# Quaternion product in a fused fp32 transformer block: four last sums joined into two, and a new order of the steps

## What is computed

```python
x = L0_attn_x
xn = _layernorm(x)
x = x + _L0_attn_ref(xn, ...) + _L0_ffn_ref(xn, Wg, Wu, Wd)      # linear attention + FFN; 8 dense experts
xn = _layernorm(x)
x = x + _L1_attn_ref(xn, ...) + _L1_ffn_ref(xn, ...)             # 4 "quaternion" layers; top-2 of 8 experts
```

```python
qk = _hamilton(_to_quaternion(q), _to_quaternion(k))
qkv_p = _hamilton(qk, _to_quaternion(v))
# _hamilton(a, b), part by part:
a0*b0 - a1*b1 - a2*b2 - a3*b3
a0*b1 + a1*b0 + a2*b3 - a3*b2
a0*b2 - a1*b3 + a2*b0 + a3*b1
a0*b3 + a1*b2 - a2*b1 + a3*b0
```

## Time and profile before

| | |
|---|---|
| median of 3 runs | 1518.19 us (1517.88 to 1524.01) |
| the profiled execution | 1522.51 us |
| its span, first to last instruction | 1520.7 us |
| mean granted clock of TensorE | 0.978 of full speed |
| PE busy | 1404.2 us, 92% of the span |
| DVE busy | 1253.9 us, 82% |
| ACT busy | 1046.8 us, 69% |
| POOL busy | 361.5 us, 24% |

### The profile page before, as it was taken

One profiled execution on the slowest core, in us unless ns is written; L12 is line 12 of the kernel. 1 busy time (PEld: TensorE's weight loads), 2 busy tenths in 40 slices (PEclk: granted clock), 3 DMA queues, 4 the chain that ended last, 5 costly groups with the idle time before them and its releaser, 6 DMA issues.

```text
span 1520.7 us, 20946 instructions
## 1 busy us (share of the span) xinstructions
PE 1404.2 (92%) x6198; PEld 994.6 (65%) x6198; DVE 1253.9 (82%) x1575; ACT 1046.8 (69%) x2413; POOL 361.5 (24%) x251
## 2 busy tenths in 40 slices
PE   6999998999999999899998899999889999999876
PEld 4767765666666666566655667656667787777653
DVE  3443467876999989999959897999899998999995
ACT  6556557666886777766887767777767686776552
POOL 0001202310131412111131410130524343543410
PEclk9999999999999999999999899999999999999989
DMA  7754455244545554534263335455546465655262
GB/s 268 264 210 150 148 176 193 70 130 138 187 144 154 165 174 138 188 116 120 96 220 119 103 106 159 127 153 163 161 148 211 129 204 176 199 169 155 68 177 83
DMA packets 111244, 238.03 MB, mean 157 GB/s; under 512 B 13207, under 2 KB 52844, under 8 KB 109644
## 3 DMA queue, kind: packets, MB, share of 16 engines
q1 hardware_dynamic: 106588, 227.31, 48.2%
q0 software_dynamic: 4544, 9.38, 1.8%
HBM read 185.59 MB, written 43.86 MB: 151 GB/s over the span
## 4 chain that ended last, share of the span: by engine, by line
PE 37%; issue 24%; DVE 16%; ACT 10%; POOL 9%; DMA 3%; SPq 0%; POOLq 0%; ACTq 0%; DVEq 0%
PE bank L1353 7%; PE bank L1341 6%; PE bank L1343 6%; PE bank L1342 6%; POOL RSTD L1016 4%; POOL ytok L1031 4%; PE bank L1530 3%; ACT ROWS L856 2%; DVE SH L1207 2%; DVE AM L1075 2%; DVE TA L1071 2%; PE bank L1448 2%; ACT ROWS L869 2%; DVE AM L1079 1%; PE bank L1442 1%
## 5 line engine op out<-in xcount | busy, mean ns | idle before, releaser
L1016 POOL TENSOR_TENSOR RSTD<-SS,power_half 128x4 f32<-128x4 f32 x96 | 156.8, 1633 | 835.3 <-ACT ROWS L856 835.2
L1353 PE MATMUL bank<-SH,WD 128*128 128x512 f32 x512 | 262.8, 595 | 2.1 <-DMA WD<-in_w_d 1.6
L1341 PE MATMUL bank<-NH,GU 128*128 128x512 f32 x512 | 246.4, 481 | 0.5 <-DVE SH L1207 0.5
L1207 DVE TENSOR_TENSOR SH<-SH,bank 128x512 f32<-128x512 f32 x256 | 172.5, 682 | 88.0 <-ACT SH L844 48.8
L1071 DVE TENSOR_TENSOR TA<-QKV 128x2048 f32<-128x2048 f32 x96 | 219.6, 2287 | 1.3
L1343 PE MATMUL bank<-NL,GU 128*128 128x512 f32 x512 | 202.3, 395 | 0.0
L1342 PE MATMUL bank<-NH,GU 128*128 128x512 f32 x512 | 202.2, 395 | 0.0
L844 ACT ACTIVATE SH<-bank 128x512 f32<-128x512 f32 x256 | 153.4, 605 | 63.8 <-PE bank L1343 61.8
L1031 POOL DMA_INDIRECT ytok<-YS,XR x78 | 118.1, 1514 | 152.2 <-ACT YS L1004 138.1
L1075 DVE TENSOR_TENSOR AM<-AM,TA 128x1024 f32<-128x1024 f32 x128 | 153.2, 1217 | 0.5
L869 ACT ACTIVATE ROWS<-bank,RSTD 128x128 f32<-128x128 f32 x384 | 109.9, 373 | 56.5 <-POOL RSTD L1016 48.6
(11 more groups left out here) (234 smaller groups left out, 2858.1 us busy)
## 6 DMA issues: line engine op xcount, KB each, us to landing
GU<-halves SPq DMA_DIRECT2D x112, 512.0 KB, 4.4
QKV<-QKV SPq DMA_DIRECT2D x32, 720.0 KB
GU<-in_w_gu SPq DMA_DIRECT2D x39, 512.0 KB
xg<-in_c_fill SPq DMA_DIRECT2D x8, 2080.0 KB
WD<-in_w_d SPq DMA_DIRECT2D x128, 128.0 KB
FC<-ready_w SPq DMA_DIRECT2D x32, 512.0 KB
WQ<-ready_w SPq DMA_DIRECT2D x32, 384.0 KB
WD<-in_w_d SPq DMA_DIRECT2D x39, 256.0 KB
```

The source lines that it names most:

```text
L1016: pool.tensor_tensor(RSTD[:], SS[:], (power_one if k[0] == "at" else power_half)[:], ALU.pow).then_inc(power_done, 1)
L1207: dve.tensor_tensor(SH[:, g % 4, :], SH[:, g % 4, :], banks[2 + g % 2][:], ALU.mult).then_inc(h_ready, 1)
L1341: pe.matmul(out, w_hi, x_hi, start=True, stop=False)
L1353: pe.matmul(banks[4][:], WD1[:, slot, :], SH[:, g % 4, :], start=first, stop=last).then_inc(down_done, 1)
```

## The change

The four one-part sums become two sums of two parts. For that, `pair`, which gives two parts of a buffer as one operand with a stride, may now walk backwards: parts 2 and 0, or 3 and 1, of `TA` are added to parts 1 and 3, or subtracted from parts 0 and 2, of `AM`. The product has 11 DVE instructions and not 13. The planner's lengths are changed for it, and every constant in `TUNE` is another; so the order of the steps on all engines is another.

```diff
-HAM, FOLD = 13, 2
+HAM, FOLD = 11, 2
...
 TUNE = {
-    "early": 169.23,
-    "norm0": (-117.36, -300.1),
-    "keys": (153.9, 106.13),
-    "kv_sum": 23.4,
-    "query": (41.25, -217.83),
-    "attn": (48.45, 18.66),
-    "norm1": (63.9, -430.46),
-    "ffn2": (142.38, -497.8),
-    "norm2": (194.13, -111.51),
-    "route": (114.57, -514.99),
-    "norm3": (-258.94, 50.46),
-    "start": (-144.04, -58.08),
-    "layer": -54.03,
...
-    "tile": (-233.31, -422.74, -201.88, 164.87, 38.59, 120.65, -166.06, -428.55),
-    "late": 189.14,
-    "pace": 1.09,
-    "prep": (-605.23, -390.98, 38.11, -347.49),
+    "early": 143.42,
+    "norm0": (63.66, 138.57),
+    "keys": (2.16, -91.96),
+    "kv_sum": 99.89,
+    "query": (-114.29, 21.92),
+    "attn": (-530.68, 60.65),
+    "norm1": (6.27, -290.36),
+    "ffn2": (61.95, 78.33),
+    "norm2": (-316.74, 372.11),
+    "route": (-253.95, -159.76),
+    "norm3": (-536.98, 101.32),
+    "start": (-212.39, -101.56),
+    "layer": 31.03,
...
+    "tile": (-148.75, -97.73, 121.33, -13.4, 82.96, -29.4, 9.24, -232.7),
+    "late": 580.17,
+    "pace": 1.4,
+    "prep": (-612.62, -227.77, -420.14, 32.1),
 }
...
-    TIMES = (2.2, 2.2, 1.13, 1.13, 2.2, 1.13, 1.13, 2.2, 0.6, 0.6, 0.6, 0.71, 2.2)
+    TIMES = (2.2, 2.2, 1.13, 1.13, 2.2, 1.13, 1.13, 2.2, 1.13, 1.13, 2.2)
...
         def pair(ap, a, b):
+            if a > b:
+                return ap[:, a:None if b == 0 else b - 1:b - a, :]
             return ap[:, a:b + 1:b - a, :]
...
             sums = {2: ((1, 2), (0, 3), ADD), 3: ((0, 3), (1, 2), SUB),
-                    5: ((2, 3), (0, 1), ADD), 6: ((0, 1), (2, 3), SUB)}
+                    5: ((2, 3), (0, 1), ADD), 6: ((0, 1), (2, 3), SUB),
+                    8: ((1, 3), (2, 0), ADD), 9: ((0, 2), (3, 1), SUB)}
...
             elif i in sums:
-                dve.wait_ge(ham, base + (2 if i < 4 else 5))
+                dve.wait_ge(ham, base + (2 if i < 4 else 5 if i < 7 else 8))
                 d, s, op = sums[i]
                 ins = dve.tensor_tensor(pair(AM, *d), pair(AM, *d), pair(TA, *s), op)
-            elif i < 12:
-                dve.wait_ge(ham, base + 8)
-                d, s, op = ((3, 0, ADD), (2, 1, SUB), (1, 2, ADD), (0, 3, SUB))[i - 8]
-                ins = dve.tensor_tensor(AM[:, d, :], AM[:, d, :], TA[:, s, :], op)
             else:
-                dve.wait_ge(ham, base + 12)
+                dve.wait_ge(ham, base + 10)
                 ins = dve.tensor_tensor(TA[:], AM[:], own(QKV[:, h, 2, :, :]), ALU.mult)
```

More of the change, by code:

```diff
@@ L145, in run @@
                 spare.remove(min(spare))
-            elif name == "ham" and key[2] == 12:
+            elif name == "ham" and key[2] == HAM - 1:
                 spare.append((at + length + 0.2, self.half[key[0:2]]))
@@ L161 @@
 TUNE = {
-    "early": 169.23,
-    "norm0": (-117.36, -300.1),
-    "keys": (153.9, 106.13),
-    "kv_sum": 23.4,
-    "query": (41.25, -217.83),
-    "attn": (48.45, 18.66),
-    "norm1": (63.9, -430.46),
-    "ffn2": (142.38, -497.8),
-    "norm2": (194.13, -111.51),
-    "route": (114.57, -514.99),
-    "norm3": (-258.94, 50.46),
-    "start": (-144.04, -58.08),
-    "layer": -54.03,
-    "each": (78.36, -392.2, -49.07, -118.46, -305.38, -191.61, -187.96, -160.42, 82.77, -138.09, -133.87, -247.32, -94.32, -175.66, -224.9, -98.81, 81.31, -178.68, -375.29, -318.68, 33.02, 31.75, -109.19, -76.99, 60.62, -281.47, 439.43, -517.99, 110.97, -417.4, -324.73, -152.28),
-    "tile": (-233.31, -422.74, -201.88, 164.87, 38.59, 120.65, -166.06, -428.55),
-    "late": 189.14,
-    "pace": 1.09,
-    "prep": (-605.23, -390.98, 38.11, -347.49),
+    "early": 143.42,
[11 more added lines that the diff above has]
+    "layer": 31.03,
+    "each": (96.86, 119.59, 76.4, 133.74, -133.42, 115.26, -319.68, -31.7, 37.4, -11.25, -83.67, -1.74, -66.3, -35.03, -122.79, -301.58, -232.74, -226.45, 16.83, -503.27, -213.27, -140.35, -409.63, -67.92, -121.82, 80.1, 48.26, 206.23, 85.94, -65.85, 624.91, -447.36),
+    "tile": (-148.75, -97.73, 121.33, -13.4, 82.96, -29.4, 9.24, -232.7),
+    "late": 580.17,
+    "pace": 1.4,
+    "prep": (-612.62, -227.77, -420.14, 32.1),
 }
@@ L329, in schedule @@
                      [("ham", (t, l, i - 1), DVE, 0.0)] if i else [("cosines", key, ACT_), ("differences", key, DVE), ("roll", key, SP, 5.0)])
-            step("fold", key, u + 1.2, [(DVE, 1.86, ("XG",), ("AM",))], [("ham", (t, l, 12), DVE, 0.0)])
+            step("fold", key, u + 1.2, [(DVE, 1.86, ("XG",), ("AM",))], [("ham", (t, l, HAM - 1), DVE, 0.0)])
             step("freq", key, u + 1.3, [(PE, 0.86, ("6",))], [("fold", key, DVE)])
```

## The result

The changed kernel takes 1535.46 us in the median of 4 runs (1533.65 to 1539.03), beside 1521.04 us of the kernel before on the same chip: a ratio of 1.0096, 95% interval 1.007 to 1.0122. Measured once more, the ratio was 1.0090 (1.0067 to 1.0114). The forecast was 1509.4 us, with a range from 1495 to 1530; the time lies above it, on the side that had 0.19.

A forecast was written before the change was run, and what follows sets the result against it. Bound: PE from 228 to 1045 us, DVE from 1045 to 1430. Profiled 1522.5 - 1.8 (joined sums) - 7 (order) = 1513.7 us; that execution lay 4.3 above the median, so 1509.4, range 1495 to 1530; slower had 0.19.

The forecast's parts named there:

- One episode's worth, -7 us: New order: gains one starved episode like that around 800 us, 4.4 us of PE standing plus 2.8 of slowed clock.
- The reading that the first tiles get ready sooner: Lower `attn`, `norm2`, `norm3` make each sequence's first tile ready for its layers sooner, favouring more layers ahead of 1045 us.
- About -16 us for a layer moved ahead: A layer moved before 1045 us lengthens the PE-bound stage by up to 12.5 us, shortens the DVE-bound one by 28.8.
- the third rival: The new order moves a whole layer ahead of the dense experts' end at 1045 us: 1500 us, chance 0.17.
- the prediction's own sign: More or fewer than 14 products behind the dense experts' end would mean layer terms, not episodes, made the difference.
- DVE sets the pace: Routed blocks, 1045 to 1430 us: DVE, busy 95%, is the bound; PE, busy 94%, has clearly less weight.
- The joined sums: DVE's last sums per product: pitch falls from 2.52 to 2.39 us, saving 0.13 us; forecast -1.8 us, between 0 and -4.2.
- the zero for the reversed walk: Sums with a reversed operand stream as fast as forward ones, no cost; at half speed, 1.07 us more per sum.
- 14 x 0.13 = 1.8 us on the engine that sets the pace: The 14 products after 1045 us save 1.8 us of DVE time, which reaches the end in full.
- "nothing" for the 18 earlier products: Before 1045 us the 18 products free 2.3 us of DVE, which has 103 us to spare: counted as nothing.
- The slower rival: A layer slips behind the dense experts, as the second tile's norm yields to all layers: 1532 us, chance 0.16.
- The planner's lengths: Planner books 0.25 us less per product, about 0.13 too short; this only makes waits, at most 4.2 us.

The follow-up runs named there:

- experiment 3: The changed kernel with all `TUNE` constants of the kernel before, the planner's new lengths kept: 1638.37 us, ratio 1.0748 to the kernel before.
- experiment 4: The changed kernel with two constants of the kernel before back (`late` 189.14, `pace` 1.09): 1593.82 us, ratio 1.0456 to the kernel before.
- experiment 9: The old lists with joined sums, but the two joined sums of q and k left out (72 us of DVE less): 1514.33 us, ratio 0.9956 to the kernel before.
- experiment 17: The changed kernel with GELU in place of SiLU in the routed blocks, for fewer function table loads on ACT: 1536.05 us, ratio 1.0096 to the kernel before.
- experiment 1: The kernel before, its lists kept, with the four sums joined into two at the place of the second and fourth: 1528.37 us, ratio 1.0021.
- experiment 10: The kernel before, its lists kept, with the four sums joined into two at the place of the first and third: 1520.23 us, ratio 1.0002.

## Why the prediction was wrong, step by step

**"One episode's worth, -7 us"** is the term that failed: the order lost 10 to 16 us where it was to gain 7. It had no row that gave its sign, and the text said so. I read the constants one by one (`late` right for the stage, `norm3` good, `norm2` bad), and experiments 3 and 4 show that this can't be done: two constants moved alone cost some 56 us against the changed kernel, and all old constants with the new lengths 100 us. What was to be had was the plan itself. The lists are made by `schedule()`, which stands in both kernels, and it plans the changed kernel 8.6 us longer, with the dense experts' end 47 us later. The prediction didn't use it. The reading that the first tiles get ready sooner may be right, as layers did move ahead, but it didn't help.

The episode that gave the 7 us was misread in one point. L1353's 1057 ns are not from the gap at 800 us: its six matmuls between 800 and 816 us took 590 to 591 ns. What ran slowly there was L1489, six matmuls in 5.09 us. The price doesn't hang on it, as it came from the granted clock of 0.65.

**"About -16 us for a layer moved ahead"** had the wrong sign. By DVE's work nearly two layers (1.9 at 28.8 us) went ahead of the cut. Behind it they brought 40.3 us, 21 a layer and not 28.8. Ahead of it they cost 52 us, 27 a layer, where I had reckoned up to 12.5 of PE: PE's busy time alone grew by 20 a layer, and its idle time, which my price left out, by 14.3 us in all. So the third rival's mechanism came true and its time did not: 1500 us was forecast for it, 1535.5 measured. By the prediction's own sign, another number of products than 14 behind the dense experts' end, it was the layer terms and not the episodes that made the difference.

**"DVE sets the pace" behind 1045 us** failed too, at a small price for the number. I took the fuller engine (95%) for the bound. Relieving DVE, PE, both, or the weight loads left the blocks' stretch between 373.9 and 378.6 us; only other lists changed it much (342 us in experiment 4). What paces it is then the way in which the fixed lists chain the engines to each other: each engine stands at the head of its list until another is done, and most of the freed time turns into waiting, as in the product of experiment 9. For that one product the chain is shown, a norm's hand-overs between PE and ACT. Which chains hold the stretch as a whole wasn't found, and ACT's share is untested, as experiment 17 didn't relieve it.

**The joined sums.** The pitch was right, 0.13 us a product, and so was the zero for the reversed walk. "14 x 0.13 = 1.8 us on the engine that sets the pace" was wrong in its second half, and "nothing" for the 18 earlier products wasn't quite right either. Behind the cut 29.1 us taken from DVE gave 3.0 (experiment 9 against 1). Ahead of it 42.1 us gave 11.7 against experiment 1 and 2.2 against experiment 10, two kernels that differ by 9.4 us in that stretch. At these rates the edit is worth 0.3 to 0.8 us, an estimate that no measurement of this kernel could confirm. Experiment 10 fits it; the 3 us that experiment 1 loses stay unexplained.

**The slower rival** has a time near the measured one, 1532 us, by the opposite mechanism (a layer slipping behind the dense experts' end). The trace refutes it: 11 products behind, not more than 14. So its nearness is luck. That the range's upper end missed by 5 us is the smaller fault.

**The planner's lengths.** I put their error of 0.13 us per product at no more than 4.2 us. As a direct stall that may hold. But the lengths also decide the order, and there the change of the same steps turned 1528 into 1638 us (experiments 1 and 3).

## What to carry to other kernels

An engine that is busy 95% of a stretch is not yet its bound: with lists fixed in advance on several engines, take work away from it (leave out instructions, keep the order) and see what the stretch gives back, before pricing a change by its throughput. Here that was a tenth to a quarter, and moving work to a stretch with idle time cost more than it saved. Constants of a planner were tuned for one set of lengths, so an edit to the steps should first be tried inside the old lists; experiment 10 shows that there was next to nothing to win. And where the order comes from a planner, run the planner before forecasting: its own ends showed this loss stage by stage, though by themselves they don't settle differences under some 10 us.

## What the runs showed of the hardware

A two-part operand of 2 x 512 columns walked from the higher part to the lower streams as fast as a forward one: 1217 ns for 1024 fp32 columns in both. Joining two 512-column instructions into one of 1024 saved some 65 ns of pitch, no more. The mean granted clock of the tail was 0.74 in experiment 4 and 0.75 in experiment 3, a mix of its levels of 1.2 and 2.4 GHz, with PE busy 59% and 62% of it; the kernel before has 0.90 behind 1430 us with 70%. One form of matmul, L1529, took 729 ns in the mean in the tail of experiment 4 and 592 ns in the blocks' stretch of the changed kernel, at 0.99. So a tail with PE often idle costs twice, once in waiting and once in slower matmuls.
